# Writing out the steps of a gather-and-sum stage with constant addresses, in a graph-attention and feed-forward kernel

## The chip, the cores and the metric

The kernel runs on one core of a Trainium2 chip. The metric is the time on the device in microseconds (us), from start to end of one execution, lower being better. Durations in what follows are those of one execution that was recorded by the hardware profiler.

## The reference

Two layers are computed one after the other on x, 3125 rows (nodes) of 1024 numbers. The first is graph attention over 50000 edges that arrive sorted by dst; the second is a quantised linear layer.

```python
xp = (layernorm(x) @ W).reshape(N, 4, 256)                 # N = 3125
e = leaky_relu(a_src[src] + a_dst[dst], 0.2)               # edges, with a loop on each node
alpha = softmax of e over the edges with the same dst      # one number per edge and head
out = segment_sum(xp[src] * alpha, dst)                    # THE STAGE THAT IS CHANGED
x = x + relu(out + bias)
x = x + quantised(layernorm(x)) @ quantised(weight).T + ffn_bias
```

## The kernel before

The work runs in stages: weights and projection (0 to some 520 us of the profile), gather-and-sum (525 to 1243 us), and the normalisation, mix and linear layer of the end (to 1558 us). Only the function `aggregate`, the gather-and-sum, is touched.

Edges are handled in steps of 256, as two halves (SUB = 2, index `u`) of 128 edges. A step works for one tile of 128 destination nodes and there are STEPS = 220 of them, numbered k. In a step:

- GpSimd (POOL) issues two indirect DMAs (L1630). Each fetches 128 rows of 4 KB (a high and a low half of 1024 numbers each) from `d_xp` in the chip's memory into a buffer `xg`. There are six pairs of buffers (XB = 6). A buffer is refilled once the matmuls that read it have counted up `mm_done`. GpSimd's 220 steps were already written out before the change.
- VectorE (DVE) makes two 128x128 one-hot matrices `hot` that say which edge belongs to which node (L1649, function `one_hots`), and the low half of the weighted one-hots `wgt` (L1657, `weights`). It reads the number of the tile from `tile_row` into a register (L1677, `value_load`), waits on three semaphores, and adds the sums of the step before to the accumulators `zsum` (L1684) and `acc` (L1685), at an address that comes from that register.
- ScalarE (ACT) makes the high half of `wgt`, four heads for each of two halves, eight ACTIVATE of 128x128 (L1704).
- TensorE (PE) runs 24 matmuls of 128 rows by 256 columns into `sum_ps` (L1732) and two small ones into `z_ps` (L1742), 26 in all, each with a weight load of its own (PEld). It waits for the gather (`arrived`, L1725), for a free sum buffer (`added`, L1727), and in each half for `high_ready` and `low_ready` (L1728).

Work runs ahead by buffers: four of `hot` (TURN), three of `wgt` (WB), three of `sum_ps` (SB), two of `z_ps`, six of `xg`.

TensorE and ScalarE run steps 0 to 215 as a loop of 18 rounds of 12 steps (ROUND = 12) and the last four written out. VectorE has its first 12 turns written out, then a loop over 17 rounds, then four turns written out. In a loop the number of the step is a register. A wait for a count that depends on it, and an operand whose address depends on it (L1649, L1657, L1677, L1704, L1742), take instructions of the engine's sequencer that compute a register, shown as FUSED_REGOPS and ALU_OP in the profile. In written-out steps these values are constants.

Of the kernel before, what the change touches and what calls it, by code (L numbers as in the profile page):

```python
# [17 lines left out]
ALU = mybir.AluOpType  # L18
# [7 lines left out]
HEADS = 4  # L26
C = D // HEADS
KC = D // P
TILES = -(-N // P)
# [5 lines left out]
SUB = 2  # L35
# [4 lines left out]
STEPS = -(-(ET + TILES - 1) // 4) * 4  # L40
KCOLS = 2 * P
KT = STEPS
# [11 lines left out]
XB = 6  # L54
# [1521 lines left out]
def aggregate(nc, maker, g):  # L1576
# [3 lines left out]
    TURN = 4  # L1580
    WB = 3
    SB = 3
    ROUND = 12
    V = 2 * HEADS
    ctx = ExitStack()
    with ctx:
# [19 lines left out]
        ROUNDS = STEPS // ROUND  # L1606
        BEHIND = range(18, TILES - 1)
        assert XB + len(BEHIND) < 18 and ROUND % XB == 0 and ROUND < 18 and STEPS - ROUNDS * ROUND == TURN and ROUND % WB == 0 and ROUND % TURN == 0
        col = lambda table, u, k, n=1: table.rearrange("p (u k) -> p u k", u=SUB)[:, u, bass.ds(k, n)]

        @block.sync
        def _(sp):
# [30 lines left out]
        @block.vector  # L1643
        def _(dve):
            def one_hots(k, j):

                dve.wait_ge(mm_done, SUB * (k + 1))
                for u in range(SUB):
                    nc.vector.tensor_scalar(hot[j][u][:, :], iota16[:, :], col(dstT, u, k), None,  # L1649
                                            ALU.is_equal).then_inc(hot_ready, 1)  # L1650

            def weights(k, j, s):
                for u in range(SUB):

                    dve.wait_ge(hot_ready, SUB * k + u + 1)
                    dve.wait_ge(mm_done, SUB * (k + 1) + u + 1)
                    nc.vector.tensor_tensor(  # L1657
                        out=wgt[s][u][:, HEADS:V, :].rearrange("p v (n b) -> p v n b", b=2),
                        in0=hot[j][u][:, :].rearrange("p (n b) -> p n b", b=2).unsqueeze(1).to_broadcast([P, HEADS, P // 2, 2]),
                        in1=numT16[:, bass.ds(u * KT + k, 1), HEADS:V, :].rearrange("p o v b -> p (o v) b").unsqueeze(2)  # L1660
                        .to_broadcast([P, HEADS, P // 2, 2]), op=ALU.mult).then_inc(low_ready, 1)

            for k in range(WB):
                one_hots(k, k)
            for k in range(WB - 1):
                weights(k, k, k)
            nc.vector.memset(zsum[:, :, :], 0.0)
            nc.vector.memset(acc[:, KC:2 * KC, :], 0.0).then_inc(ends_cleared, 1)
            dve.wait_ge(ends_cleared, 1)

            def turn(k, j, last=False):

                if not last:
                    one_hots(k + 3, (j + 3) % TURN)
                if not last or j + 2 < TURN:
                    weights(k + 2, (j + 2) % TURN, (j + 2) % WB)
                t = dve.value_load(tile_row[0:1, bass.ds(k, 1)], min_val=0, max_val=TILES - 1)  # L1677

                dve.wait_ge(mm_done, SUB * (k + 1 + TURN))
                dve.wait_ge(added, k + SB)  # L1680
                dve.wait_ge(z_added, k + 2)
                s_acc = acc[:, bass.ds(t, 1), :].rearrange("p o n -> p (o n)")
                z_acc = zsum[:, bass.ds(t, 1), :].rearrange("p o n -> p (o n)")
                nc.vector.tensor_tensor(out=z_acc, in0=z_ps[j % 2][:, 0:V], in1=z_acc, op=ALU.add).then_inc(z_added, 1)  # L1684
                nc.vector.tensor_tensor(out=s_acc, in0=sum_ps[j % SB][:, :], in1=s_acc, op=ALU.add).then_inc(added, 1)  # L1685

            for j in range(ROUND):
                turn(j, j)
            dve.wait_ge(cleared, len(BEHIND))
            with dve.Fori(1, ROUNDS) as i:  # L1690
                for j in range(ROUND):
                    turn(ROUND * i + j, j)
            for j in range(TURN):
                turn(ROUNDS * ROUND + j, j, last=(j > 0))

        @block.scalar
        def _(act):
            def weights(k, j):
                for u in range(SUB):

                    act.wait_ge(hot_ready, SUB * k + u + 1)
                    act.wait_ge(mm_done, SUB * (k + 1) + u + 1)
                    for h in range(HEADS):
                        last = nc.scalar.activation(wgt[j % WB][u][:, h, :], hot[j % TURN][u][:, :], ACT.Copy,  # L1704
                                                    scale=col(numT[:, h, :], u, k))
                    last.then_inc(high_ready, 1)

            with act.Fori(0, ROUNDS) as i:
                for j in range(ROUND):
                    weights(ROUND * i + j, j)  # L1710
            for j in range(TURN):
                weights(ROUNDS * ROUND + j, j)

        @block.tensor
        def _(pe):

            pe.sem_inc(mm_done, SUB * TURN)  # L1717
            pe.sem_inc(added, SB)
            pe.sem_inc(z_added, 2)

            def step(k, j, n):
                s, z, x, w = j % SB, j % 2, xg[j % XB], wgt[j % WB]
                pe.wait_ge(arrived[j % XB], n)

                pe.wait_ge(added, k + 1)  # L1725
                for u in range(SUB):
                    pe.wait_ge(high_ready, SUB * k + u + 1)  # L1727
                    pe.wait_ge(low_ready, SUB * k + u + 1)  # L1728
                    for h in range(HEADS):

                        for n, (a, b) in enumerate(((0, 0), (0, 1), (1, 0))):
                            last = nc.tensor.matmul(  # L1732
                                sum_ps[s][:, h * C:(h + 1) * C], w[u][:, a * HEADS + h, :],
                                x[u][:, b, h * C:(h + 1) * C],
                                start=(u == 0 and h % 2 == 0 and n == 0), stop=(u == SUB - 1 and h % 2 == 1 and n == 2),
                                skip_group_check=True)
                    if u == 0:
                        last.then_inc(mm_done, 1)

                pe.wait_ge(z_added, k + 1)  # L1740
                for u in range(SUB):
                    last = nc.tensor.matmul(z_ps[z][:, 0:V], hot[j % TURN][u][:, :],  # L1742
                                            numT16[:, bass.ds(u * KT + k, 1), :, 0].rearrange("p o v -> p (o v)"),
                                            start=(u == 0), stop=(u == SUB - 1))
                last.then_inc(mm_done, 1)

            per = ROUND // XB
            with pe.Fori(0, ROUNDS) as i:
                for j in range(ROUND):
                    step(ROUND * i + j, j, 16 * SUB * (per * i + j // XB + 1))  # L1750
            for j in range(TURN):
                step(ROUNDS * ROUND + j, j, 16 * SUB * (ROUNDS * per + 1))


def finish(nc, maker, g):
# [429 lines left out]
```

## Time and profile before

| what | value |
|---|---|
| median of 3 runs | 1566.23 us (1562.82 to 1567.08) |
| span of the profiled execution | 1558.2 us |
| own time of the profiled execution beside its span | not listed; the median less the span is 8.0 us |
| TensorE busy over the span | 1366.1 us, 88% |
| VectorE, ScalarE, GpSimd busy | 1119.8 us (72%), 1038.5 us (67%), 686.3 us (44%) |
| TensorE's matmuls, and as many weight loads | 10462 |
| first and last matmul of L1732 | start at 525.5 and at 1242.9 us |

The span runs from the first to the last recorded instruction of the kernel. Engine busy times overlap one another. A line such as L1732 is a line of the kernel's file. PE is TensorE's matmul, PEld its weight load; a letter q behind an engine's name marks an instruction that its sequencer runs, which is not counted as busy time. A wait is named by what ended it; "issue" means that nothing in the profile explains it.

### The profile page before, as it was taken

The page shows a single profiled execution, that of the slowest core. Times are in us where ns is not written, and L with a number is a line of the kernel's source. Part 1 is how long each engine was busy: PE and PEld are TensorE (multiplying, and loading weights), DVE is VectorE, ACT ScalarE, POOL GpSimd, SP SyncE. Part 2 cuts the span into 40 slices and gives each one's busy share as a digit, 9 for nine tenths or more (in the row PEclk, how much of TensorE's full clock was granted, in tenths as well). Part 3 has the DMA queues.
Part 4 walks back from the last instruction along what each step waited for, and adds up shares of the span by engine and source line. Part 5 has one row for each costly group of instructions (what it writes and reads, how often), then busy time and mean ns, then how long its engine had stood idle before and what let it go on. Part 6 is the DMA issues. An engine that isn't in the chain of part 4 may idle for free. (4 is left out here: it accounts for less than half of the span.)

```text
span 1558.2 us, 35658 instructions
## 1 busy us (share of the span) xinstructions
PE 1366.1 (88%) x10462; PEld 936.5 (60%) x10462; DVE 1119.8 (72%) x2486; ACT 1038.5 (67%) x2349; POOL 686.3 (44%) x629
## 2 busy tenths in 40 slices
PE   7998588989998598888888888888898859999998
PEld 5785244544443377777777777777777725454543
DVE  7887499889834576777677676767676787777771
ACT  3667488884455477777777777777777656566652
POOL 1002510111263576666666666666666334444441
PEclk9999799999999799999999999999999969999999
DMA  6774375533453788888888898888888856777752
GB/s 237 258 271 151 109 276 190 184 135 137 165 204 153 286 264 299 288 276 295 289 277 295 298 324 298 289 272 302 284 274 298 312 164 173 187 188 181 198 141 46
DMA packets 113831, 360.98 MB, mean 232 GB/s; under 512 B 23966, under 2 KB 24750, under 8 KB 113506
## 3 DMA queue, kind: packets, MB, share of 16 engines
q0 software_dynamic: 69408, 223.51, 45.0%
q1 hardware_dynamic: 40994, 135.71, 25.0%
q10 hardware_dynamic: 3360, 0.91, 0.2%
q8 instruction: 36, 0.59, 0.2%
q14 instruction: 33, 0.27, 0.1%
HBM read 312.36 MB, written 72.85 MB: 247 GB/s over the span
## 5 line engine op out<-in xcount | busy, mean ns | idle before, releaser
L1732 PE MATMUL sum_ps<-xg,wgt 128*128 128x256 f16 x5280 | 632.3, 276 | 93.5 <-issue 77.3
L1704 ACT ACTIVATE wgt<-hot,tables 128x128 f16<-128x128 f16 x1760 | 533.6, 388 | 192.0 <-PE sum_ps L1732 64.0
L1732 PEld LDWEIGHTS sum_ps<-xg,wgt 128*128 128x128 f16 x5280 | 501.6, 99 | 188.8 <-issue 128.9
L1630 POOL DMA_INDIRECT xg<-d_xp,tables x428 | 431.8, 1009 | 259.7 <-issue 96.6
L1512 PE MATMUL xp_ps<-acc 128*128 128x512 f16 x1152 | 271.8, 385 | 15.4 <-issue 5.9
L2134 PE MATMUL fmm_ps<-xg,tables 128*128 128x512 f16 x1200 | 265.7, 382 | 4.0 <-DVE tables L1963 4.0
L1685 DVE TENSOR_TENSOR acc<-sum_ps,acc 128x1024 f32 x220 | 267.8, 1217 | 0.3 <-issue 0.3
L2134 PEld LDWEIGHTS fmm_ps<-xg,tables 128*128 128x128 f16 x1200 | 117.9, 98 | 142.4 <-issue 7.9
L1512 PEld LDWEIGHTS xp_ps<-acc 128*128 128x128 f16 x1152 | 108.8, 99 | 138.6 <-issue 19.8
L1684 DVE TENSOR_TENSOR zsum<-z_ps,zsum 128x8 f32 x220 | 35.6, 162 | 209.5 <-remote 68.8
L1657 DVE TENSOR_TENSOR wgt<-hot,tables 128x512 f16<-128x512 f16 x440 | 167.0, 424 | 3.0 <-issue 3.0
L1865 POOL TENSOR_TENSOR tables<-tables,finv 128x1024 f32<-128x1024 f32 x24 | 45.9, 1913 | 132.0 <-DVE finv L1951 132.0
L1649 DVE TENSOR_SCALAR hot<-iota,tables 128x128 f16<-128x128 f16 x440 | 93.2, 272 | 4.4 <-PEq L1717 4.3
L1022 POOL TENSOR_TENSOR acc<-acc,q_inv 128x1024 f32<-128x1024 f32 x8 | 17.3, 2158 | 175.3 <-DVE q_inv L1145 175.3
L1489 PEld LDWEIGHTS gat_ps<-table,oh 128*128 128x128 f16 x790 | 41.5, 98 | 59.9 <-ACT oh L1413 21.3
L1489 PE MATMUL gat_ps<-table,oh 128*128 128x100 f16 x790 | 48.4, 209 | 33.0 <-DVEq L1100 28.4
L1092 DVE TENSOR_TENSOR prod<-gat_ps,mask 128x500 f32<-128x500 f32 x79 | 53.2, 673 | 27.9 <-remote 18.2
L1381 ACT ACTIVATE acc<-xp_ps,half_scale 128x1024 f16<-128x1024 f32 x24 | 26.7, 1113 | 67.9 <-PE xp_ps L1512 56.9
L1975 DVE SCALAR_TENSOR_TENSOR tables<-ftr_ps,tables 128x1024 f16<-128x1024 f32 x24 | 29.4, 1224 | 54.1 <-ACT tables L2077 54.1
L1413 ACT ACTIVATE oh<-tables,back_lane 128x1280 f16<-128x1280 bf16 x40 | 54.0, 1351 | 14.3 <-remote 14.3
L1114 DVE SCALAR_TENSOR_TENSOR acc<-xp_ps,half_scale,acc 128x1024 f16<-128x1024 f32 x24 | 30.7, 1281 | 43.1 <-ACT acc L1382 26.1
L1871 POOL TENSOR_TENSOR tables<-fq,fscale 128x1024 f32<-128x1024 fp8e4 x24 | 54.1, 2254 | 15.1 <-ACT fq L2068 15.1
(306 smaller groups left out, 1543.3 us busy)
## 6 DMA issues: line engine op xcount, KB each, us to landing
d_xnT<-acc SPq DMA_DIRECT2D x25, 512.0 KB, 2.9
tables<-d_lo SPq DMA_DIRECT2D x40, 320.0 KB
own_row<-d_own SPq DMA_DIRECT2D x25, 512.0 KB
wdT<-in_x_dram SPq DMA_DIRECT2D x24, 512.0 KB, 4.7
acc<-d_xnT SPq DMA_DIRECT2D x24, 512.0 KB
d_xp<-acc SPq DMA_DIRECT2D x24, 512.0 KB
d_own<-acc SPq DMA_DIRECT2D x24, 512.0 KB
xr<-in_x_dram SPq DMA_DIRECT2D x24, 512.0 KB
```

The source lines that it names most:

```text
L1092: return own.mark(nc.vector.tensor_tensor(out=prod[:, :, :, :], in0=gat_ps[u % 2][:, 0:UCOLS * V].rearrange("p (c h t) -> p c h t", c=UCOL ...
L1413: nc.scalar.activation(oh[at][:, :], digits[at], ACT.Abs, bias=back_lane[:, :]).then_inc(oh_ready, 1)
L1489: last = nc.tensor.matmul(gat_ps[u % 2][:, c * V:(c + 1) * V], oh[b % LB][:, col], table[a][:, :], start=(c == 0 and a == 0), stop=(c == U ...
L1512: done = nc.tensor.matmul(xp_ps[j][:, cols], xh[j][:, a, c, :], w16[:, c, b, cols], start=False, stop=(c == KC - 1 and a == 1), skip_group ...
L1630: nc.gpsimd.indirect_dma_start(out=xg[s][u][:, :, :].rearrange("p a n -> p (a n)"), out_offset=None, in_=d_xp, in_offset=bass.IndirectOffs ...
L1649: nc.vector.tensor_scalar(hot[j][u][:, :], iota16[:, :], col(dstT, u, k), None, ALU.is_equal).then_inc(hot_ready, 1)
L1657: nc.vector.tensor_tensor(out=wgt[s][u][:, HEADS:V, :].rearrange("p v (n b) -> p v n b", b=2), in0=hot[j][u][:, :].rearrange("p (n b) -> p ...
L1685: nc.vector.tensor_tensor(out=s_acc, in0=sum_ps[j % SB][:, :], in1=s_acc, op=ALU.add).then_inc(added, 1)
L1704: last = nc.scalar.activation(wgt[j % WB][u][:, h, :], hot[j % TURN][u][:, :], ACT.Copy, scale=col(numT[:, h, :], u, k))
L1732: last = nc.tensor.matmul(sum_ps[s][:, h * C:(h + 1) * C], w[u][:, a * HEADS + h, :], x[u][:, b, h * C:(h + 1) * C], start=(u == 0 and h % ...
L1871: nc.gpsimd.tensor_tensor(out=blocks(xn[t % XN]), in0=blocks(q8[t % 2][:, :]), in1=spread(scale[t % XN][:, :]), op=ALU.mult).then_inc(xq_r ...
L2134: return nc.tensor.matmul(mm_ps[t % 2][:, cols], xqT[t % 2][:, a, c, :], wd[c][:, b, cols], start=False, stop=last, skip_group_check=True)
```

## The change

In `aggregate` the loops of VectorE, ScalarE and TensorE are replaced by Python loops over all 220 steps, which write every step out. The step number k is then a constant everywhere: the buffer indices become k % XB, k % WB and so on, the addresses of `dstT`, `numT`, `numT16` and `tile_row` become constants, and so do the counts waited for. The only register address left is that of the accumulators of VectorE, which depends on data (`value_load`). Operations, their order on each engine, their sizes, the buffers and the semaphores are the same. The wait for `cleared` stays ahead of VectorE's turn 12. GpSimd and the queue of SyncE are not touched.

```diff
-        col = lambda table, u, k, n=1: table.rearrange("p (u k) -> p u k", u=SUB)[:, u, bass.ds(k, n)]
+        col = lambda table, u, k: table[:, u * KT + k:u * KT + k + 1]
...
-                        in1=numT16[:, bass.ds(u * KT + k, 1), HEADS:V, :].rearrange("p o v b -> p (o v) b").unsqueeze(2)
+                        in1=numT16[:, u * KT + k, HEADS:V, :].unsqueeze(2)
...
-            def turn(k, j, last=False):
-
-                if not last:
-                    one_hots(k + 3, (j + 3) % TURN)
-                if not last or j + 2 < TURN:
-                    weights(k + 2, (j + 2) % TURN, (j + 2) % WB)
-                t = dve.value_load(tile_row[0:1, bass.ds(k, 1)], min_val=0, max_val=TILES - 1)
+            def turn(k):
+
+                if k + 3 < STEPS:
+                    one_hots(k + 3, (k + 3) % TURN)
+                if k + 2 < STEPS:
+                    weights(k + 2, (k + 2) % TURN, (k + 2) % WB)
+                t = dve.value_load(tile_row[0:1, k:k + 1], min_val=0, max_val=TILES - 1)
...
-            for j in range(ROUND):
-                turn(j, j)
-            dve.wait_ge(cleared, len(BEHIND))
-            with dve.Fori(1, ROUNDS) as i:
-                for j in range(ROUND):
-                    turn(ROUND * i + j, j)
-            for j in range(TURN):
-                turn(ROUNDS * ROUND + j, j, last=(j > 0))
+            for k in range(STEPS):
+                if k == ROUND:
+                    dve.wait_ge(cleared, len(BEHIND))
+                turn(k)
...
-            with act.Fori(0, ROUNDS) as i:
-                for j in range(ROUND):
-                    weights(ROUND * i + j, j)
-            for j in range(TURN):
-                weights(ROUNDS * ROUND + j, j)
+            for k in range(STEPS):
+                weights(k, k)
...
-            def step(k, j, n):
-                s, z, x, w = j % SB, j % 2, xg[j % XB], wgt[j % WB]
-                pe.wait_ge(arrived[j % XB], n)
+            def step(k):
+                s, z, x, w = k % SB, k % 2, xg[k % XB], wgt[k % WB]
+                pe.wait_ge(arrived[k % XB], 16 * SUB * (k // XB + 1))
...
-                    last = nc.tensor.matmul(z_ps[z][:, 0:V], hot[j % TURN][u][:, :],
-                                            numT16[:, bass.ds(u * KT + k, 1), :, 0].rearrange("p o v -> p (o v)"),
+                    last = nc.tensor.matmul(z_ps[z][:, 0:V], hot[k % TURN][u][:, :], numT16[:, u * KT + k, :, 0],
...
-            with pe.Fori(0, ROUNDS) as i:
-                for j in range(ROUND):
-                    step(ROUND * i + j, j, 16 * SUB * (per * i + j // XB + 1))
-            for j in range(TURN):
-                step(ROUNDS * ROUND + j, j, 16 * SUB * (ROUNDS * per + 1))
+            for k in range(STEPS):
+                step(k)
```

## Rows read from the trace of the kernel before

**Rows 1.** The page: span, and the chain that ended last by engine.

```profile
span 1558.2 us, 35658 instructions
PE 18%; DVE 1%; ACT 0%; issue 0%; DVEq 0%
```

**Rows 2.** Windows: start and end, length, busy time with counts, granted clock, DMA share, GB/s.

```profile
60.00:120.00 60.00, 60.00 (x642) 48.38 (x641) 51.96 (x160) 37.79 (x64) 0.00 (x0) 1.00 0.77 271
...
570.90:1232.00 661.10, 583.73 (x5308) 490.45 (x5306) 465.59 (x1220) 493.15 (x1627) 409.53 (x407) 0.99 0.85 290
1232.00:1243.00 11.00, 10.82 (x107) 9.64 (x105) 8.59 (x19) 6.29 (x22) 0.00 (x0) 1.00 1.01 381
1268.00:1550.00 282.00, 282.00 (x1391) 139.50 (x1390) 201.07 (x413) 169.50 (x230) 118.90 (x72) 0.99 0.65 164
```

**Rows 3.** Groups by line, 570.9 to 1232 us: busy us, mean ns, idle before them.

```profile
L1732 PE MATMUL sum_ps<-xg,wgt 128*128 128x256 f16 x4898 | 583.0, 274 | 72.6 <-issue 70.7 <-ACT wgt L1704 0.8
L1704 ACT ACTIVATE wgt<-hot,tables 128x128 f16<-128x128 f16 x1627 | 493.3, 388 | 168.7 <-PE sum_ps L1732 61.2 <-remote 48.9 <-PE z_ps L1742 36.3
...
L1630 POOL DMA_INDIRECT xg<-d_xp,tables x407 | 410.4, 1008 | 251.3 <-issue 91.7 <-PE sum_ps L1732 72.3 <-PE z_ps L1742 70.9
L1685 DVE TENSOR_TENSOR acc<-sum_ps,acc 128x1024 f32 x204 | 248.4, 1217 | 0.3 <-issue 0.3
```

**Rows 4.** Waits, 570.9 to 1232 us: total us, times, longest us.

```profile
PEld sum_ps L1732 <- issue: 106.2, 168, 1.3
POOL xg L1630 <- issue: 91.7, 294, 1.3
```

**Rows 5.** Timeline of the loop: start us, length us, engine, operation, count, idle before.

```profile
813.28 1.58 PE L1732 MATMUL sum_ps<-xg,wgt 128*128 128x256 f16 x13
815.03 0.38 PE L1732 MATMUL sum_ps<-xg,wgt 128*128 128x256 f16 x2 [0.17 <-issue]
815.78 1.15 PE L1732 MATMUL sum_ps<-xg,wgt 128*128 128x256 f16 x9 [0.37 <-issue]
...
816.82 2.78 PE L1732 MATMUL sum_ps<-xg,wgt 128*128 128x256 f16 x24
...
819.49 1.91 PE L1732 MATMUL sum_ps<-xg,wgt 128*128 128x256 f16 x16
```

**Rows 6.** Sequencers of ScalarE and VectorE, 917.0 to 919.3 us: min/median/max ns.

```profile
L1704 ACTq FUSED_REGOPS  x3: 14/686/700, 917.1 to 917.9; - x3
...
L1657 DVEq FUSED_REGOPS  x2: 75/384/694, 917.1 to 917.9; - x2
...
L1677 DVEq ALU_OP  x1: 698/698/698, 918.6 to 918.6; - x1
```

**Rows 7.** Sequencer instructions of the loops by line, 570.9 to 1232 us.

```profile
L1704 ACTq FUSED_REGOPS  x1616: 14/46/700, 571.8 to 1227.4; - x180
...
L1742 PEldq FUSED_REGOPS  x408: 60/64/69, 571.9 to 1230.2; - x136
...
L1728 PEldq EVENT_SEMAPHORE  x407: 51/51/51, 572.4 to 1231.5; - x136
...
L1727 PEldq FUSED_REGOPS  x203: 42/42/42, 572.3 to 1228.6; - x102
...
L1748 PEldq COMPARE_BRANCH  x17: 83/215/215, 607.5 to 1230.4; - x17
```

**Rows 8.** The same of steps already written out, on TensorE and ScalarE, then VectorE.

```profile
L1728 PEldq EVENT_SEMAPHORE  x7: 51/51/51, 1232.2 to 1240.4; - x7
...
L1702 ACTq EVENT_SEMAPHORE  x6: 17/17/17, 1229.0 to 1235.4; - x6
...
L1656 DVEq EVENT_SEMAPHORE  x12: 21/21/21, 542.9 to 556.6; - x12
```

**Rows 9.** The page: the DMA queue that carries TensorE's instructions, packets and MB.

```profile
q8 instruction: 36, 0.59, 0.2%
```

**Rows 10.** A window of 10 us of the loop, same columns as Rows 2.

```profile
900.00:910.00 10.00, 9.12 (x89) 8.03 (x87) 7.68 (x22) 7.98 (x27) 6.50 (x8) 1.00 1.02 402
```

More of the change, by code:

```diff
@@ L1683, in turn @@
                 z_acc = zsum[:, bass.ds(t, 1), :].rearrange("p o n -> p (o n)")
-                nc.vector.tensor_tensor(out=z_acc, in0=z_ps[j % 2][:, 0:V], in1=z_acc, op=ALU.add).then_inc(z_added, 1)
-                nc.vector.tensor_tensor(out=s_acc, in0=sum_ps[j % SB][:, :], in1=s_acc, op=ALU.add).then_inc(added, 1)
-            for j in range(ROUND):
-                turn(j, j)
-            dve.wait_ge(cleared, len(BEHIND))
-            with dve.Fori(1, ROUNDS) as i:
-                for j in range(ROUND):
-                    turn(ROUND * i + j, j)
-            for j in range(TURN):
-                turn(ROUNDS * ROUND + j, j, last=(j > 0))
+                nc.vector.tensor_tensor(out=z_acc, in0=z_ps[k % 2][:, 0:V], in1=z_acc, op=ALU.add).then_inc(z_added, 1)
+                nc.vector.tensor_tensor(out=s_acc, in0=sum_ps[k % SB][:, :], in1=s_acc, op=ALU.add).then_inc(added, 1)
+            for k in range(STEPS):
+                if k == ROUND:
+                    dve.wait_ge(cleared, len(BEHIND))
+                turn(k)
         @block.scalar
@@ L1741, in step @@
                 for u in range(SUB):
-                    last = nc.tensor.matmul(z_ps[z][:, 0:V], hot[j % TURN][u][:, :],
-                                            numT16[:, bass.ds(u * KT + k, 1), :, 0].rearrange("p o v -> p (o v)"),
+                    last = nc.tensor.matmul(z_ps[z][:, 0:V], hot[k % TURN][u][:, :], numT16[:, u * KT + k, :, 0],
                                             start=(u == 0), stop=(u == SUB - 1))
                 last.then_inc(mm_done, 1)
-            per = ROUND // XB
-            with pe.Fori(0, ROUNDS) as i:
-                for j in range(ROUND):
-                    step(ROUND * i + j, j, 16 * SUB * (per * i + j // XB + 1))
-            for j in range(TURN):
-                step(ROUNDS * ROUND + j, j, 16 * SUB * (ROUNDS * per + 1))
+            for k in range(STEPS):
+                step(k)
 def finish(nc, maker, g):
```

## The prediction

> **What bounds the kernel now.** I read the page first. The chain that ended last [rows 1] covers only the last 300 us or so and lies wholly behind the changed stage, so it doesn't help. What can be read is the stage itself: it ends when TensorE's last step ends, and the next stage follows at once, so time saved in the steps is time saved in the kernel. Next came the windows, which show the stretch in which all three loops run, 570.9 to 1232 us [rows 2], then the groups, waits and timeline of that stretch [rows 3 to 5].
>
> That stretch is 661.1 us for 204 steps (L1685 runs once a step [rows 3]), 3.24 us a step. Where TensorE isn't interrupted a step takes 2.67 us: one begins at 816.82, the next at 819.49 [rows 5]. So 0.57 us a step, 116 us in all, are lost. They aren't lost to any engine that feeds TensorE: of the idle time before L1732, 70.7 us are put down to "issue" and 0.8 us to ScalarE [rows 3], and PEld has 106.2 us of "issue" in 168 pieces of up to 1.3 us [rows 4]. The timeline shows what they are: in the middle of a step, where no wait stands in the code, TensorE stops, passes one or two matmuls, stops again (815.03, then 815.78), and then runs at full speed [rows 5]. ScalarE, VectorE and GpSimd wait for TensorE afterwards [rows 3], so they follow it.
>
> What stops it? In some of these stops the other engines show that it isn't TensorE alone. From 917.1 to 919.3 us the sequencers of ScalarE and VectorE take 686 to 700 ns for register instructions whose median in the stretch is 46 ns [rows 6, 7], and they do so while TensorE stands too. Such an instruction has no operand in memory and waits for nobody. Something that all engines share holds every instruction for about 0.7 us at a time. It doesn't come with a high DMA load alone: in the last four steps the DMA runs at 381 GB/s and TensorE is busy 10.82 of 11 us. Nor does it come with a high rate of instructions alone: from 60 to 120 us TensorE passes 10.7 matmuls a us with as many weight loads, more than the 8.0 of the loop, and stands nowhere, at 271 GB/s [rows 2]. It takes both, and of the two the change lowers the rate of instructions.
>
> **The change part by part.** Instructions a step, from the counts over 204 steps. TensorE: 26 matmuls and 26 weight loads, two FUSED_REGOPS of L1742 (408), two waits of L1728 (407), two instructions for L1727 (203 of them this form, and an ALU_OP each) [rows 7] and one for L1725, 59 in all. Its steps already written out have none on L1742, two waits on L1728 [rows 8] and one on L1727, so 55. ScalarE: eight ACTIVATE (1627), eight FUSED_REGOPS (1616) [rows 3, 7] and two for L1702, 18; written out it needs eight and two waits [rows 8], 10. VectorE: six operations and some 14 sequencer instructions, 20; in its turns written out before, from 541 to 560 us, I count 14, two of them waits of L1656 (12 in six turns [rows 8]). GpSimd: 4, unchanged. The sum goes from about 102 to 83, by 19%.
>
> What that is worth depends on who counts against whom. If only TensorE's own instructions count, the step follows 59 to 55: 3.24 x 55 / 59.3 = 3.01 us. If all count alike, it is 3.24 x 83 / 102 = 2.64 us, less than TensorE's own 2.67, which then is the end. I take 2.84 us, the middle of 3.01 and 2.67: [rows 6] speak for a thing that all share, but nearly all the stops that I see show TensorE alone with the others merely idle, and more steps a us also means more DMA, which I counted as the other half of the cause. Both ends stay in the range. The gain is (3.24 - 2.84) x 204 = 82 us.
>
> The floors behind it: GpSimd needs 2 x (1.008 + 0.30) = 2.62 us a step (1008 ns for one of L1630 [rows 3]; 91.7 us of "issue" in 294 pieces is 0.31 each [rows 4]). The gathers move 2 x 128 rows x 4 KB = 1.05 MB a step, which at the 402 GB/s of a 10 us window [rows 10] is 2.61 us. ScalarE is busy 493.3 us for 204 steps, 2.42 us, with its ACTIVATE overlapping. VectorE 465.6 / 204 = 2.28 us. All lie below 2.67, though closely, so nothing takes away the gain before 2.67, and nothing can give more than 116 us.
>
> The branches: TensorE's is 17 times 215 ns [rows 7]. I cost them at nothing, since matmuls queued ahead cover 0.2 us; if the cover were gone they'd be 4 us. The register instructions of VectorE and ScalarE lie beside their engines' work and are worth nothing in themselves, as both wait for TensorE. VectorE's `value_load` stays. The 12 steps ahead of 570.9 us took 45.4 us and have the ramp of the stage in them; I count no gain there, and up to 13 us (down to 2.67 a step) at the low end. The last four steps and all other stages are as before: 0. No wait is added and no queue is passed.
>
> Of loops the Trainium skill has a rule of its own (Runtime: NRT & Kernel Launch, Instruction fetch mechanics): a taken branch to a place outside the blocks that the sequencer holds must fetch them first, which is why full unrolling is preferred. That would make the loops' ends the cost. By it the gain would be at most 17 stops of the longest length seen, 1.3 us, 22 us in all. The trace disagrees: PEld stands 168 times in the stretch [rows 4] for 17 branches.
>
> The median of the runs is 1566.2, the profiled span 1558.2; the 8.0 us around it stay. 1566.2 - 82 = **1484 us**.
>
> **The rivals.**
>
> *TensorE's instructions alone count, or the DMA gives way first.* Step 3.01 us, gain 47 us, 1519 us. The DMA comes to the same: if it can't hold 402 GB/s but 350, a step is 3.0 us. For it: the stops begin and end with TensorE's instructions. Against it: [rows 6].
>
> *The stops vanish.* Step 2.67 to 2.72 us, 106 to 129 us with the first 12 steps, 1437 to 1460 us. For it: the last four steps, written out on TensorE and ScalarE, have none at 381 GB/s [rows 2]. Against it: GpSimd issues nothing there, and 11 us are few.
>
> *The stops don't depend on register instructions.* They may follow the matmuls or time. The step stays at 3.24 us and the time at 1566 us, or, if each of TensorE's instructions bears its share of the 116 us, 7% of it goes, 8 us, 1558 us. For it: they come about every second step, so the matmul count fits as well as any other.
>
> On that point the Trainium skill (NOTIFIC — the notification-queue block, The write path) says that the block through which instruction records leave an engine holds the producers when its inner queue is full, and gathers four records into a write; that would make the stops a price per recorded instruction, and by the shared count above give 1450 to 1484 us. The same page (Constraints, capacities, measured rates) reports that a record costs the engine no cycles at the rates it measured, by which there would be no gain, 1566 us. No row of the trace before names the recorder.
>
> *The code itself becomes late: slower.* TensorE's instructions come in packets by a DMA queue, 36 of them, 0.59 MB [rows 9]. Of its 2 x 10462 matmuls and loads TensorE runs 216 x 52 in the loop and 9,700 outside, so a packet holds some 270 of them. 204 steps more of 55 instructions are 11,200, some 42 packets, and VectorE and ScalarE get their own. They share the DMA with gathers that fill it to 85% on average and to 102% at times [rows 2, 10]. If a packet holds TensorE for 1.3 us, the longest stop seen [rows 4], and the old stops stay, the stage is 42 x 1.3 = 55 us longer: 1621 us. The point from which it decides is the gain of 82 us divided by 42, 2 us a packet. Against it: from 1268 to 1550 us TensorE runs straight code without one idle us [rows 2], though at a DMA share of 0.65; and GpSimd's 220 steps are straight code in this very stage, with no wait for issue over 1.3 us [rows 4].
>
> **How the numbers follow.** Forecast, 1465 to 1510 us: 0.33. Stops gone, below 1465: 0.17. TensorE's count or the DMA, 1510 to 1540: 0.20. A small gain, 1540 to 1561: 0.05. No change: 0.12. Slower: 0.13. A measurement of this kernel tells about 0.3% (5 us) from no change. Faster is then 0.75, same 0.12, slower 0.13. The range reaches from 1448, within the case of no stops, to 1570: below it lie some 0.07, above it about 0.12.
>
> **What would show it.** Right: no FUSED_REGOPS on L1704's, L1649's and L1742's successors; some 83 instructions a step; PEld's "issue" before the sum matmuls well under 106 us; GB/s of the stage above 320; GpSimd busy nearly without a break. Wrong: the same 0.57 us a step of "issue" with the register instructions gone (the stops aren't theirs); TensorE waiting for `xg` (the DMA is the end); stops at an even distance of some 270 instructions (the code is late). A DMA that can't hold 390 GB/s would take half of the gain.

## The result, and the profile after

| what | before | after |
|---|---|---|
| median | 1566.62 us (1562.82 to 1567.08, 4 runs) | 1552.00 us (1549.80 to 1553.21, 4 runs) |
| ratio after to before, 95% interval | | 0.9909 (0.9893 to 0.9925) |
| span of the profiled execution | 1558.2 us | 1550.0 us |
| own time of that execution | not listed | 1551.72 us |
| instructions recorded | 35658 | 31610 |

The changed kernel is faster by 14.6 us, 0.9%, where 82 us were forecast. It was compared with the kernel before three times more, and gave 0.9915 (0.9898 to 0.9932), 0.9942 (0.9925 to 0.9959) and 0.9914 (0.9897 to 0.9932). The mean of the four ratios is 0.9920, a gain of 12.5 us. The occasions differ: beside the four comparisons the kernel before took 1566.6, 1567.1, 1567.1 and 1580.7 us, and the ratio is taken each time on one chip.

The page of the kernel after, its span and the queue that carries TensorE's instructions, answers to [rows 1, 9]:

```profile
span 1550.0 us, 31610 instructions
...
q8 instruction: 79, 1.29, 0.3%
```

The same windows as in [rows 2], for the kernel after. The columns are length, busy time with counts of PE, PEld, DVE, ACT and POOL, granted clock, DMA share, GB/s:

```profile
570.90:1224.00 653.10, 577.55 (x5303) 486.22 (x5302) 464.72 (x1225) 493.94 (x1632) 410.14 (x407) 0.99 0.86 295
1224.00:1235.00 11.00, 11.00 (x109) 9.86 (x108) 8.32 (x19) 6.11 (x21) 0.00 (x0) 1.00 1.01 390
60.00:120.00 60.00, 60.00 (x629) 48.16 (x628) 52.07 (x154) 38.66 (x63) 0.00 (x0) 1.00 0.78 268
```

204 steps took 661.1 us before [rows 2] and 653.2 us after (the group views below run from step 12, at 571.6 us, to step 216, at 1224.8): 3.24 and 3.20 us each. The difference of 8 us is nearly the whole of the 8.2 us between the two spans. The other 6 us of the gain in the medians lie between executions: 1.7 us stand around the span of after, and if as many stood around the 1558.2 us of before, that execution took about 1560 us, less than any of the four runs in the median.

The groups by line and the waits of the kernel after, 571.6 to 1224.8 us, answer to [rows 3, 4]:

```profile
L1725 PE MATMUL sum_ps<-xg,wgt 128*128 128x256 f16 x4898 | 576.4, 273 | 70.7 <-issue 67.4 <-DVE wgt L1657 1.1 <-ACT wgt L1700 0.2
L1700 ACT ACTIVATE wgt<-hot,tables 128x128 f16<-128x128 f16 x1632 | 494.5, 388 | 159.2 <-remote 70.9 <-PE z_ps L1735 48.8 <-PE sum_ps L1725 22.4
...
L1630 POOL DMA_INDIRECT xg<-d_xp,tables x407 | 410.1, 1008 | 242.9 <-issue 94.9 <-PE sum_ps L1725 78.7 <-PE z_ps L1735 67.7
L1685 DVE TENSOR_TENSOR acc<-sum_ps,acc 128x1024 f32 x204 | 248.4, 1218 | 0.9 <-issue 0.9
```

```profile
PEld sum_ps L1725 <- issue: 103.4, 160, 1.4
...
POOL xg L1630 <- issue: 94.9, 298, 2.7
```

This is what decided. The register instructions of the loops are gone, but PEld still stands 160 times for "issue", 103.4 us in all, where it stood 168 times and 106.2 us [rows 4]. The stops stayed. What went is 8 us of them.

The instructions of the sequencers by line, the same stretch, kernel after (count, minimum/median/maximum ns), answer to [rows 7, 8]:

```profile
L1698 ACTq EVENT_SEMAPHORE  x408: 17/17/17, 573.4 to 1224.2; - x136
...
L1656 DVEq EVENT_SEMAPHORE  x408: 21/21/21, 574.1 to 1222.8; - x136
...
L1720 PEldq EVENT_SEMAPHORE  x204: 51/51/51, 572.5 to 1223.1; - x102
...
L1721 PEldq EVENT_SEMAPHORE  x408: 51/51/51, 572.6 to 1224.4; - x136
```

ScalarE has two waits a step beside its eight ACTIVATE (10 in all), TensorE three beside its 52 (55), VectorE 14 as counted before, GpSimd 4. That makes 83 a step, as forecast. So the instructions went to just the extent planned, and their effect was mis-sized.

The timeline of the kernel after around one stop (start, length, engine, operation, count, idle before it) answers to [rows 5, 6]. It shows all engines at once:

```profile
816.95 1.00 POOL L1630 DMA_INDIRECT xg<-d_xp,tables  x1 [0.30 <-issue]
817.17 0.75 DVE L1657 TENSOR_TENSOR wgt<-hot,tables 128x512 f16<-128x512 f16 x2
...
817.45 0.27 PE L1725 MATMUL sum_ps<-xg,wgt 128*128 128x256 f16 x1 [0.30 <-issue]
818.87 1.80 PE L1725 MATMUL sum_ps<-xg,wgt 128*128 128x256 f16 x15 [1.15 <-issue]
...
819.04 2.15 ACT L1700 ACTIVATE wgt<-hot,tables 128x128 f16<-128x128 f16 x7 [1.47 <-remote]
819.23 0.17 DVE L1684 TENSOR_TENSOR zsum<-z_ps,zsum 128x8 f32 x1 [1.31 <-remote]
```

The last instruction to begin ahead of the stop is the second of the two of L1657, at 817.51 us; the next on any engine begins at 818.87. ScalarE and VectorE have been idle for 1.47 and 1.31 us when they start again.

### The profile page after: what moved, and what is told of

It is laid out like the page before. It is cut to its first block and busy times, and to the rows that moved or that the text cites. A ratio compares the mean times of both kernels' runs of the same rounds, so it can differ in the third digit from the quotient of the medians.

```text
span 1550.0 us, 31610 instructions
## 1 busy us (share of the span) xinstructions
PE 1360.2 (88%) x10462; PEld 932.7 (60%) x10462; DVE 1116.8 (72%) x2485; ACT 1038.3 (67%) x2349; POOL 685.2 (44%) x629
## 5 line engine op out<-in xcount | busy, mean ns | idle before, releaser
L1657 DVE TENSOR_TENSOR wgt<-hot,tables 128x512 f16<-128x512 f16 x440 | 166.4, 419 | 0.0
```

What stands on the lines that cost most here:

```text
L1657: nc.vector.tensor_tensor(out=wgt[s][u][:, HEADS:V, :].rearrange("p v (n b) -> p v n b", b=2), in0=hot[j][u][:, :].rearrange("p (n b) -> p ...
```

## The experiments

The theory at the start was the one of the prediction: something shared holds all engines, and it takes instructions and DMA traffic together. The runs took the parts away one at a time. Except where said, each is the changed kernel with one edit, and is measured beside the kernel before on the same chip. The kernels that leave out or replace gathers or products ran once on each occasion, the others 6 to 12 times.

**No gathers.** From step 6 on nothing is fetched, and the waits for the rows ask only for the first fill of each buffer.

```diff
-                pe.wait_ge(arrived[k % XB], 16 * SUB * (k // XB + 1))
+                pe.wait_ge(arrived[k % XB], 16 * SUB)
...
-                gather(k % XB, lambda u: srcT[:, u * KT + k:u * KT + k + 1], k)
```

> The changed kernel with the gathers of steps 6 to 219 left out, so that TensorE works on the rows of the first six steps again and again; TensorE, VectorE and ScalarE run the same instructions at the same addresses. If the stops of TensorE in the middle of a step need the DMA traffic or GpSimd's work, they vanish: a step goes from 3.20 to about 2.67 us and the kernel from 1552 to about 1435 us. If they come from the number of instructions on TensorE alone, whatever the DMA does, the step stays near 3.20 us and the kernel near 1550.

Measured: 1440.52 us, the kernel before 1579.24 us there. The window from 600 to 1100 us (columns as above), first of the changed kernel as first profiled, then of this run:

```profile
600.00:1100.00 500.00, 441.58 (x4050) 371.48 (x4048) 354.58 (x935) 377.51 (x1247) 313.88 (x312) 0.99 0.86 295
600.00:1100.00 500.00, 500.00 (x4873) 448.34 (x4871) 439.08 (x1125) 457.99 (x1500) 0.00 (x0) 1.00 0.02 6
```

TensorE is busy 500.00 of 500 us. Every stop in that window is gone with the gathers, at 83 - 4 instructions a step.

**Half the bytes.** The gathers stay, each row has 2 KB in place of 4.

```diff
-                        out=xg[s][u][:, :, :].rearrange("p a n -> p (a n)"), out_offset=None, in_=d_xp,
+                        out=xg[s][u][:, :, :].rearrange("p a n -> p (a n)") if k is None else xg[s][u][:, 0, :], out_offset=None,
+                        in_=d_xp if k is None else d_xp.rearrange("r (a n) -> (r a) n", a=2),
```

> The changed kernel with each gather from step 6 on fetching rows of 2 KB in place of 4 KB (the high half of xg alone is filled, from other rows), so GpSimd issues as many descriptors and the bytes are halved. If the stops follow the bytes that move, most of them vanish, step near 2.7 us, kernel near 1440 us. If they follow GpSimd's descriptors, step near 3.2 us, kernel near 1550 us.

Measured: 1564.73 us on the same chip. The same window, then the wait of that stretch:

```profile
600.00:1100.00 500.00, 437.30 (x4009) 367.56 (x4008) 351.67 (x928) 372.19 (x1233) 311.70 (x309) 0.99 0.53 149
```

```profile
PEld sum_ps L1726 <- issue: 79.5, 120, 1.4
```

GpSimd's DMA queue over the whole execution (packets, MB, share), changed kernel and this run:

```profile
q0 software_dynamic: 69408, 223.51, 45.0%
```

```profile
q0 software_dynamic: 42016, 123.89, 30.0%
```

The DMA share of the window fell to 0.53 and the rate to 149 GB/s, the queue's packets fell with the bytes, and TensorE is busy 437 of 500 us as in the changed kernel (441.58). Neither the bytes nor the packets are the second half of the cause. This refutes the reading in the prediction that more steps a us would bring more stops by their DMA.

**Plain transfers in place of gathers.** SyncE's queue moves the same 4 KB rows into the same buffers, two transfers of 128 rows a step. GpSimd issues nothing, and the rows are not those asked for.

```diff
+                for u in range(SUB):
+                    if k >= XB:
+                        sp.wait_ge(mm_done, SUB * (k + TURN - XB) + u + 1)
+                    r = (SUB * k + u) % TILES * P
+                    sp.dma_start(xg[k % XB][u][:, :, :].rearrange("p a n -> p (a n)"), d_xp[r:r + P, :]).then_inc(arrived[k % XB], 16)
...
-                gather(k % XB, lambda u: srcT[:, u * KT + k:u * KT + k + 1], k)
```

> The changed kernel with each gather replaced by a plain DMA of the same 128 rows of 4 KB (fixed rows) from SyncE's queue: as many bytes into the same buffers with the same waits, no descriptors made by GpSimd. If what stops TensorE is the packets that move, the stops stay: step near 3.2 us, kernel within 1% of the changed kernel. If it is GpSimd's making of descriptors, they vanish: step near 2.7 us, some 110 us less.

Measured: 1435.19 us, the kernel before 1567.12 us. Window 600 to 1100 us:

```profile
600.00:1100.00 500.00, 500.00 (x4872) 447.67 (x4870) 439.11 (x1124) 458.00 (x1500) 0.00 (x0) 1.00 1.02 401
```

At a DMA share of 1.02 and 401 GB/s there is no stop. So what it takes is GpSimd's gathers as such, not their bytes. Two things changed together here, the queue and the indirect addresses; plain transfers issued by GpSimd were not run, so which of the two counts isn't shown.

**More instructions, on TensorE and on ScalarE.** Waits that are satisfied already are put between the heads. The 30 waits more a step are 12 instructions more in the trace (95 a step in place of 83).

```diff
+                        if h:
+                            for _ in range(5):
+                                pe.wait_ge(low_ready, SUB * k + u + 1)
```

> The changed kernel with 12 more waits a step on TensorE, each already fulfilled, between its matmuls: 67 instructions a step in place of 55, nothing else. If the stops are a price per instruction of TensorE, 0.535 us for 55, the step gets 0.117 us longer, 26 us in all, kernel near 1578 us. If they are a price per instruction of all engines, 0.535 us for 83, it is 0.077 us a step, 17 us, near 1569 us. If they go by matmuls or by time, no more than what 12 x 51 ns cost TensorE's queue where it is empty, 1552 to 1557 us.

> The changed kernel with 12 more waits a step on ScalarE, each already fulfilled, between its ACTIVATE: 22 instructions a step in place of 10, nothing else. If all engines' instructions share the price, 0.077 us a step and 17 us in all, near 1569 us. If TensorE's alone count, or the matmuls or time, nothing: 1550 to 1554 us, since ScalarE waits for TensorE anyway.

Measured beside a kernel before of 1579.24 us: on TensorE 1579.53 us, ratio 1.0001 (0.9991 to 1.0011); on ScalarE (the same with `act` and `mm_done`) 1576.91 us, ratio 0.9982 (0.9972 to 0.9992). The changed kernel was not run on that chip. Against its mean ratio of 0.9920, 1566.6 us there, that is 12.9 and 10.3 us more; with its lowest and highest ratio, 0.9909 and 0.9942, it is 9 to 15 and 7 to 12 us. Twelve instructions cost about the same on either engine, and ScalarE's own 12 waits of some 17 ns have slack: it is not TensorE that pays for its own instructions, the price is shared. The theory of TensorE's count alone falls.

**The change in its two parts.** The changed kernel again, then only TensorE written out (of the diff of the change, the lines of its `step` alone), then only VectorE and ScalarE (all the other lines).

> The changed kernel itself once more, as the base for the other runs of this group, since kernels on different chips differ by some 1%. Ratio to the kernel before near 0.991 as measured, 0.35 of its 1% within any theory.

> The kernel before with only TensorE's steps written out; VectorE and ScalarE keep their loops. If the price is one for every instruction whatever its engine, the change took 19 of 102 a step for 14.6 us, 0.77 us each, and TensorE's part is 4.3 of them: 3 us, ratio 0.998. If TensorE's alone counted, all of the gain would be here: 0.991. If the branches of TensorE's loop were what cost, also 0.991.

> The changed kernel with TensorE's steps put back into the loop of before; VectorE and ScalarE stay written out. By the price for every instruction: 14.4 of the 18.7 instructions a step go, 11 us, ratio 0.993. If TensorE's alone counted: no gain, 1.000.

Measured beside 1567.12 us: 1554.19 us, ratio 0.9915 (0.9898 to 0.9932); TensorE alone 1564.57 us, 0.9984 (0.9971 to 0.9997); the others alone 1558.33 us, 0.9949 (0.9933 to 0.9965). So 2.5 us come from TensorE's 4 instructions and 18 branches, and 8.8 us from the 14 of ScalarE and VectorE, two engines that have slack. The parts sum to 11.3 of 12.9 us, within the intervals. TensorE's part alone has an interval of 0.5 to 4.5 us.

**An execution without stops.** Four further kernels ran together: more instructions beside plain transfers, one gather a step, fewer products, and a kernel with fewer waits. Their edits are shown below, where the same kernels come again; the first is the one with plain transfers and both kinds of extra waits.

> The kernel with plain transfers in place of the gathers (1435.2 us) with 15 more waits a step on TensorE and 15 or fewer on ScalarE that are all satisfied already (five ahead of each head but the first, in each half; 30 on either engine a step). The rows summed are not those that the reference asks for. Theory A (an instruction only has a price while GpSimd issues gathers, because the stops are the price): no stop in the middle of the stage and a time within 5 us of 1435, unless an engine's own queue of waits becomes longer than TensorE's work. Rival B (each instruction costs 1.2 us for each one more in a step, whatever the gathers do, as the 12 more on TensorE and the 12 more on ScalarE did): 1435 plus at least 30 x 1.2 = 36 us, over 1470.

> The changed kernel with the second gather of each step left out from step 6 on (half the descriptors, half the bytes; the second half's rows are those of the first six steps). Halving the bytes alone did not move the time. Theory A (a stop needs GpSimd making descriptors and comes when its supply and all engines' instructions together pass a rate): no stop, or nearly none, and a time of 1437 to 1460 us on a chip where the kernel before takes 1567. Rival B (the stop comes whenever a gather is issued, in proportion to the gathers): half of the 115 us of stops is left, some 1495 us. Rival C (a stop depends on the count of instructions alone, once any gather runs): 1545 or more.

> The changed kernel without the product of the high weight with the low part of the row (8 of TensorE's 24 wide products of a step left out, 16 left; 66 to 68 instructions of all engines a step in place of 83). TensorE's own work falls from 2.67 to about 1.8 us a step. GpSimd's 2.62 us of gathers a step and the DMA engines' 2.61 stay. Theory A (stops come when instructions and descriptors together pass a rate): with GpSimd's 2.62 as the bound and 67 instructions in it the rate is 25.6 an us, the same as now with stops (83 in 3.205 us, 25.9), so few stops are left: step 2.62 to 2.75 us, total 1430 to 1460 us. Rival B (each gather pair brings a stop of 0.57 us a step whatever else runs): step 2.62 + 0.57 = 3.19, total some 1550.

> The changed kernel with the waits left out that others imply: VectorE's two waits on TensorE ahead of its weights (the one-hot of the next step has waited for more), one wait in place of two for the one-hots on VectorE and on ScalarE, and one in place of two for the low weights on TensorE: 5 instructions fewer a step, 78 in place of 83. Theory A (each instruction of a step, on any engine, costs 0.6 to 1.2 us of the whole): 3 to 6 us below the changed kernel, a ratio to the kernel before of 0.987 to 0.989 where the changed kernel has 0.991. Rival B (the waits that went cost nothing, only the loops' register instructions did): 0.991, and later if waiting for both low weights ahead of the first product delays TensorE.

Measured: 1410.61, 1408.10, 1425.82 and 1416.87 us. They don't answer the questions put to them, because the kernel before itself took 1415.78 us here (1412.91 to 1417.60 in 15 runs), 151 us less than elsewhere. The kernel with fewer waits, two gathers a step and the real rows, from 600 to 1100 us, then its gathers from 540 to 1085 us:

```profile
600.00:1100.00 500.00, 495.00 (x4817) 443.60 (x4815) 433.02 (x1104) 447.71 (x1464) 373.44 (x363) 1.00 0.96 356
```

```profile
L1630 POOL DMA_INDIRECT xg<-d_xp,tables x408 | 419.4, 1028 | 126.7 <-issue 122.5 <-PE z_ps L1742 3.5 <-PE sum_ps L1732 0.6
```

The step is 2.70 us and GpSimd issues one gather after the other, 1028 ns each with the 0.30 us between two that it has everywhere. No wait of PEld for "issue" is left in that stretch. The stops, then, are not in the program: the same gathers run without them on one occasion and with them on five others. Against the profiled execution of before (span 1558.2, here 1413.7 us), 110 of the 144 us lie behind the start of step 12 and in this stage. Step 12 begins at 536.6 us in place of 570.9 [rows 2], so the other 34 us lie ahead of it; where they come from was not looked into. The kernel with fewer waits has a ratio of 1.0013 (1.0004 to 1.0022) to the kernel before here: where nothing stops, its 23 instructions fewer a step bring nothing. The changed kernel itself was not among the four. What makes the difference is open. It does not seem to be the chip: the record gives chip number 13 for these runs and for those of the next section, six minutes later, where the kernel before took 1567.05 us again.

**The same questions where the stops are.** Three of the kernels again, under the same chip number, with the changed kernel beside them; the kernel before took 1567.05 us.

```diff
-                    dve.wait_ge(hot_ready, SUB * k + u + 1)
-                    dve.wait_ge(mm_done, SUB * (k + 1) + u + 1)
+                    if k < WB - 1:
+                        dve.wait_ge(mm_done, SUB * (k + 1) + u + 1)
+                        dve.wait_ge(hot_ready, SUB * (k + 1))
+                    elif u == 0 and k + 1 < STEPS:
+                        dve.wait_ge(hot_ready, SUB * (k + 1))
...
-                    act.wait_ge(hot_ready, SUB * k + u + 1)
+                    if u == 0:
+                        act.wait_ge(hot_ready, SUB * (k + 1))
...
+                pe.wait_ge(low_ready, SUB * (k + 1))
                 for u in range(SUB):
                     pe.wait_ge(high_ready, SUB * k + u + 1)
-                    pe.wait_ge(low_ready, SUB * k + u + 1)
```

> The changed kernel once more, beside a kernel before that may take 1416 us, as on the chip of the last four runs, or some 1567, as on those of the runs before them. Theory A (the change gains only what it takes out of the stops of all engines): on a chip with no stops (kernel before about 1416) the ratio to the kernel before is 0.998 to 1.003, and a step takes 2.70 us in either kernel; on a chip with the stops it is 0.991 again. Rival B (the gain comes from the loops' register instructions, stops or not): 0.991 on either.

> The changed kernel with 5 instructions fewer a step (the waits that others imply), 78 in place of 83. Theory A (each instruction of a step on any engine costs 0.6 to 1.2 us of the whole where the stops are): 3 to 6 us below the changed kernel of the same chip if the kernel before takes some 1567 us there, ratio 0.987 to 0.989; equal to the changed kernel within 2 us if it takes 1416. Rival B (waits satisfied already cost nothing where they go, only where they are added): equal to the changed kernel on either chip.

Changed kernel 1557.00 us (1555.30 to 1559.21), ratio 0.9942 (0.9925 to 0.9959). The kernel with fewer waits 1552.02 us (1548.82 to 1553.83), ratio 0.9907 (0.9890 to 0.9924). The trace of the latter has 79 instructions a step, four fewer (two of the waits shared one), and they bring 5.0 us, with no overlap between the two sets of runs. Against the changed kernel's mean ratio, 0.9920, it is 2 us. So it is a little faster than the changed kernel in this one direct comparison; where nothing stops it loses 0.1% to the kernel before.

The plain transfers with more waits, and the single gather:

```diff
-                for u in range(SUB):
+                for u in range(SUB if k is None else 1):
...
-                pe.wait_ge(arrived[k % XB], 16 * SUB * (k // XB + 1))
+                pe.wait_ge(arrived[k % XB], 16 * (SUB + k // XB))
```

> Plain transfers in place of the gathers, with 15 waits more a step on TensorE and 15 on ScalarE, all satisfied already. The rows summed are not those that the reference asks for. Theory A (an instruction has a price only beside GpSimd's gathers): 1433 to 1440 us if the kernel before takes 1567 us on the chip, and 1410 again if it takes 1416. Rival B (each instruction has its price on such a chip whatever GpSimd does): over 1460 us where the kernel before takes 1567.

> The second gather of each step left out from step 6 on: half the descriptors and bytes; the second half's rows are old ones. On a chip where the kernel before takes some 1567 us: theory A (stops come when gathers and instructions together pass a rate): 1437 to 1460; rival B (in proportion to the gathers): some 1495; rival C (one gather or two a step, the stops are the same): 1545 or more. Where the kernel before takes 1416 us: 1408 again.

Measured: 1434.51 and 1439.66 us. The windows from 600 to 1100 us, the plain transfers first:

```profile
600.00:1100.00 500.00, 498.48 (x4852) 446.86 (x4850) 437.23 (x1122) 457.14 (x1493) 0.00 (x0) 1.00 1.02 400
```

```profile
600.00:1100.00 500.00, 500.00 (x4870) 448.36 (x4869) 439.28 (x1124) 457.88 (x1500) 232.06 (x188) 1.00 0.61 181
```

Beside plain transfers 24 instructions more a step cost nothing: 1434.51 against 1435.19 us. Without a gather such a kernel passes some 105 instructions in 2.68 us (SyncE's two issues included), 39 a us, unhindered; the changed kernel is held at 83 in 3.20 us, 26 a us. And one gather a step leaves TensorE busy 500.00 of 500 us. Half the stops at half the gathers, rival B, is refuted. The queue's packets are about those of the run with half rows, which had its stops:

```profile
q0 software_dynamic: 38592, 123.86, 31.5%
```

An obvious doubt is whether these single runs without stops were executions of the other kind, like those around 1416 us, by chance. Their traces say no. The first matmul of the stage starts at 500.0 to 502.6 us in the four executions of that occasion, and at 525.5 us before and 526.0 us after. It starts at 529.9 us without gathers, at 528.0 and 525.8 us with plain transfers, and at 528.0 us with one gather. And the same two kernels took 1410.61 and 1408.10 us there, against 1434.51 and 1439.66 us here.

**Fewer products.** The last pair: the changed kernel, and that kernel with 16 of TensorE's 24 wide products of a step.

```diff
-                        for n, (a, b) in enumerate(((0, 0), (0, 1), (1, 0))):
+                        for n, (a, b) in enumerate(((0, 0), (1, 0))):
...
-                                start=(u == 0 and h % 2 == 0 and n == 0), stop=(u == SUB - 1 and h % 2 == 1 and n == 2),
+                                start=(u == 0 and h % 2 == 0 and n == 0), stop=(u == SUB - 1 and h % 2 == 1 and n == 1),
```

> The changed kernel beside the kernel before. On a chip where the kernel before takes some 1567 or 1579 us, theory A (19 instructions fewer a step, each at 0.5 to 1.2 us of the whole) gives a ratio between 0.991 and 0.994, as in the three comparisons so far; on one where it takes 1416 us theory A gives 0.998 to 1.003, rival B (the loops' register instructions cost something of their own) 0.991.

> 8 of TensorE's 24 wide products of a step left out (high weight by low part of the row), 66 to 68 instructions of all engines a step in place of 83, both gathers kept. Where the kernel before takes 1416 us this kernel took 1425.8, waiting for the gathered rows. Where it takes some 1567: theory A (a stop comes when instructions and descriptors together pass a rate) gives few stops and 1425 to 1470 us; rival B (two gathers a step bring 0.57 us of stops a step, whatever the engines execute) some 1550 us.

Measured beside 1580.73 us: the changed kernel 1568.45 us, ratio 0.9914 (0.9897 to 0.9932), and 1540.62 us with fewer products. From 600 to 1100 us, and the wait of that stretch:

```profile
600.00:1100.00 500.00, 358.27 (x2859) 282.90 (x2860) 360.90 (x959) 383.93 (x1276) 317.45 (x319) 0.90 0.87 301
```

```profile
PEld sum_ps L1725 <- issue: 164.4, 191, 1.8
```

TensorE has 1.8 us of work a step here, and a step still takes 3.17 us (2.69 us with the same kernel where nothing stops). It stands for "issue" more than ever, 164.4 us, since it has more time to spare. With 67 instructions in 3.17 us, 21 a us, the stops are there. So there is no rate of instructions below which they vanish, as I had expected in theory A: they vanish when a gather goes. Rival B, some 1550 us, came nearest: with two gathers a step the stops stay, whatever the engines execute, and the time is 10 us below that rival's.

**What remains.** One account fits these runs where the stops are. It is a model fitted to them, not a thing seen in a trace: a pair of gathers and the instructions of a step draw on one supply, and the step is the longer of TensorE's 2.67 us and what the supply needs. The instructions' share comes from the pairs of runs:

| edit | instructions a step | time, us | us for one instruction a step |
|---|---|---|---|
| the change, mean of four | -19 | -12.5 | 0.7 |
| TensorE alone | -4 | -2.5 | 0.6 |
| VectorE and ScalarE alone | -14 | -8.8 | 0.6 |
| waits on TensorE | +12 | +12.9 | 1.1 |
| waits on ScalarE | +12 | +10.3 | 0.9 |
| waits merged | -4 | -5.0 (-2 against the mean) | 0.5 to 1.2 |
| fewer products | -16 | -27.8 | 1.7 |

Over 220 steps 0.5 to 1.2 us is 2 to 6 ns an instruction; the last line, from one run, has TensorE's lower clock (0.90) and other work in it, and 8 of its 27.8 us lie ahead of step 12. In the steps behind that it went from 3.26 us to 3.17, which is 6 ns an instruction. At 4 ns the 83 instructions are 0.33 us of the 3.20, and the two gathers the other 2.87, 1.4 each. By that a step with one gather needs 1.4 + 0.3 = 1.7 us of the supply, below 2.67, and shows no stop, as measured. That this supply is one path, and which, is only argued; it wasn't measured by itself, and a kernel between one and two gathers a step wasn't run.

## Why the prediction was wrong

*What bounds the kernel.* Right: the 0.57 us a step lie in stops that no engine's work explains, they hold all engines, and time saved in a step is time of the kernel. Wrong in part: "It takes both" a high DMA load and a high rate of instructions. It takes two gathers a step from GpSimd, whatever they move, and no rate of instructions tried was low enough to end the stops; instructions only lengthen them. The comparison that misled was the last four steps, without stops at 381 GB/s [rows 2]. I noted under the second rival that GpSimd issues nothing there and set it aside; this was the row that named the cause.

*The count.* Right: 102 to 83, engine by engine.

*What the count is worth.* This step failed. I scaled the whole step of 3.24 us by the count, for TensorE's count to 3.01 us and for all to 2.64 us, and took 2.84, a gain of 0.40 us a step. Measured were 0.04 us in the profiled pair and 12.5 / 220 = 0.06 us in the mean of the medians. Scaling the step says that instructions are all that the shared resource carries. At the 2 to 6 ns that the pairs of runs give for one, the 83 are 0.2 to 0.5 us of the 3.20, a tenth or so, and by the account above the gathers are the rest. Both bounds came from the same assumption, so the range between them didn't bound the unknown cost. The other bound stood under the third rival: each instruction bears its share of the 116 us of stops. With all engines counted, that is 19%, 22 us; with TensorE's 7%, 8 us. The 12.5 us lie between. Of the signs named ahead, two for being right failed (PEld's "issue" at 103.4 us and not well under 106, 295 GB/s and not above 320), and the first for being wrong came: 0.53 us of lost time a step with the register instructions gone.

*The floors.* Right where nothing stops: a step took 2.70 us, and 2.69 where TensorE had only 1.8 us of work, by GpSimd and the DMA. They played no part elsewhere.

*The branches.* Priced at nothing to 4 us. TensorE's part of the change, 18 branches and 4 instructions, brought 2.5 us, and four instructions at the others' 0.6 us are 2.5 us, so next to nothing is left for branches; the interval of 0.5 to 4.5 us allows some 2 us for them. The rule cited there, that a taken branch waits for its code (the Trainium skill, Runtime: NRT & Kernel Launch, Instruction fetch mechanics), gave up to 22 us; the runs bear out no cost of that size.

*The rivals.* 1552 us lies in the case of a small gain, 1540 to 1561 us, which had a chance of 0.05 and no working of its own but the 1558 us of the third rival. Taking the third rival as a whole, stops that don't depend on register instructions, it came nearest. The late code was refuted: 43 packets more came (79 against 36 [rows 9]; 42 were estimated), and no wait for them can be seen. With all stops away, in the run with plain transfers, the same 79 packets leave TensorE busy 500 of 500 us at a DMA share of 1.02. The vanished stops are a real state of this stage, reached without the gathers, and once with them by the kernel before and by the kernel with fewer waits, but not by this edit.

Of the recorder's two rules (the Trainium skill, NOTIFIC — the notification-queue block, The write path, and Constraints, capacities, measured rates) the runs agree with the second where there are no gathers (24 instructions more a step cost nothing, at 39 a us), and a price for each instruction beside gathers, 2 to 6 ns, would look like the first. They don't tell a record from its instruction: no run was made without the recording, so whether it is the recorder that holds the engines, and whether the stops are there without it, is open.

## What to carry to other kernels

When a shared resource stops all engines, find out who fills it before pricing the share that an edit removes: take each user away by itself (no gathers, half the bytes, the same bytes from another queue, twelve instructions more), and scale the time by the measured price of one unit, never the whole time by the count. Writing out these loops was worth 0.7 us for each instruction a step and next to nothing for the branches. With half of the gathers, or with plain transfers from another queue, 115 us and more of 1557 went, on rows that aren't those asked for; whether the right rows could be had so wasn't tried.

## What the runs showed of the hardware

- Two indirect DMAs of 128 rows a step from GpSimd hold all engines, TensorE included, for some 0.5 us of each 3.2 us step. One a step holds none (1439.7 us), nor do two plain transfers of the same bytes from SyncE's queue (1435.2 us at 401 GB/s). Halving the bytes, which took two fifths of the queue's packets too, left the stops (1564.7 us where the kernel before took 1579.2).
- Beside these gathers an instruction lengthens the step by 2 to 6 ns, on whichever engine it is, even a wait that is satisfied at once on an engine with slack. Without the gathers 24 more a step cost nothing (1434.5 us).
- The same kernel took 1566.6 to 1580.7 us in five comparisons and 1415.8 us in one, under a chip number that also gave 1567.1 us. The difference is these stops and some 34 us ahead of step 12. A change that acts on such stops has a ratio that holds only where they are.
